# Even 11-step slots for the node work, and register reads and gathers issued one block earlier, in a graph and mixture-of-experts kernel

## What is computed

```
x = x + gat(layernorm(x), src, dst)     # 12 heads, softmax over incoming edges
x = x + moe(layernorm(x))               # 4 experts, the best one for each node
x = x + gcn(layernorm(x), edge_index)   # two graph convolutions
x = x + ffn(layernorm(x))               # 768 -> 384 -> 768, tanh gelu
```

## Time and profile before

| | us |
|---|---|
| median of 3 runs | 1054.82 |
| lowest and highest | 1052.24, 1055.24 |
| the profiled execution's own time | 1055.24 |
| its span in the profile | 1053.4 |
| outside the span | 1.84 |
| TensorE busy | 980.8 (93%) |
| VectorE busy | 607.2 (58%) |
| ScalarE busy | 287.9 (27%) |
| GpSimd busy | 60.0 (6%) |

### The profile page before, as it was taken

One profiled execution on the slowest core, in us unless ns is written; L12 is line 12 of the kernel. 1 busy time (PEld: TensorE's weight loads), 2 busy tenths in 40 slices (PEclk: granted clock), 3 DMA queues, 4 the chain that ended last, 5 costly groups with the idle time before them and its releaser, 6 DMA issues. The chain is left out here.

```text
span 1053.4 us, 15653 instructions
## 1 busy us (share of the span) xinstructions
PE 980.8 (93%) x5652; PEld 793.7 (75%) x5652; DVE 607.2 (58%) x1261; ACT 287.9 (27%) x782; POOL 60.0 (6%) x114
## 2 busy tenths in 40 slices
PE   7999998999999999958599994999999999999997
PEld 4777676999999999946366652666997557888785
DVE  8887897999999999985322225552111112232331
ACT  2444344454444554213011110221111112200100
POOL 2000000000000000012122211000000000000000
PEclk9999998999999999979699996999999999999999
DMA  6000010000000001528552236114200005000001
GB/s 156 2 1 1 5 49 1 24 26 24 24 34 37 24 24 43 127 81 283 174 177 92 89 147 197 57 44 162 71 1 1 0 1 146 1 30 30 28 3 60
DMA packets 25528, 65.26 MB, mean 62 GB/s; under 512 B 5720, under 2 KB 9572, under 8 KB 25344
## 3 DMA queue, kind: packets, MB, share of 16 engines
q1 hardware_dynamic: 22833, 54.13, 16.5%
q0 software_dynamic: 2080, 10.23, 2.9%
q10 hardware_dynamic: 559, 0.16, 0.1%
HBM read 47.74 MB, written 16.76 MB: 61 GB/s over the span
## 5 line engine op out<-in xcount | busy, mean ns | idle before, releaser
L809 PE MATMUL O<-X,masks 125*125 125x264 f32 x1200 | 279.6, 333 | 2.9 <-DVE masks L954 2.9
L806 PE MATMUL O<-X,CSR 125*125 125x132 f32 x1080 | 245.1, 227 | 0.0
L809 PEld LDWEIGHTS O<-X,masks 125*125 125x125 f32 x1200 | 222.2, 187 | 3.1 <-issue 3.1
L954 DVE SCALAR_TENSOR_TENSOR masks<-a2b,NA,CSR 125x375 fp32r<-125x375 f32 (+1 forms) x360 | 212.5, 645 | 8.3 <-PE O L809 5.9
L806 PEld LDWEIGHTS O<-X,CSR 125*125 125x125 f32 x1080 | 205.2, 190 | 0.0
L1879 DVE SCALAR_TENSOR_TENSOR UL<-pw,dinv,UH 125x768 fp32r<-125x768 f32 x20 | 20.4, 1018 | 111.4 <-ACT UH L1802 111.4
L1659 PE MATMUL pw<-W 128*125 128x384 f32 x240 | 81.6, 498 | 1.0 <-ACT W L1795 1.0
L424 PE MATMUL pc<-ohs_a,ohd 125*125 125x512 f16 x375 | 77.9, 347 | 1.6 <-DVE ohs_a L629 1.6
L1659 PE MATMUL pw<-region,xr_or_h 128*125 128x384 f32 x240 | 77.6, 486 | 0.0
L151 POOL TENSOR_TENSOR rstd<-rstd,minus_half 125x1 f32<-125x1 f32 x40 | 25.4, 636 | 843.8 <-DVEq L145 843.8
L1659 PEld LDWEIGHTS pw<-W 128*125 128x125 f32 x240 | 45.5, 193 | 32.3 <-issue 3.7
(11 more groups left out here) (237 smaller groups left out, 1384.3 us busy)
## 6 DMA issues: line engine op xcount, KB each, us to landing
a2b<-a_rows SPq DMA_DIRECT2D x12, 610.4 KB
W<-in_L_ffn_W SPq DMA_DIRECT2D x4, 1152.0 KB, 5.9
WM<-in_L_ffn_W SPq DMA_DIRECT2D x4, 1152.0 KB, 8.4
xr_or_h<-in_x SPq DMA_DIRECT2D x10, 336.0 KB
region<-in_x SPq DMA_DIRECT2D x2, 1680.0 KB
z_rows<-region SPq DMA_DIRECT2D x10, 336.0 KB
region<-y_rows SPq DMA_DIRECT2D x10, 336.0 KB
x_rows<-xr_or_h SPq DMA_DIRECT2D x10, 336.0 KB
```

The lines of the kernel that those rows point to most:

```text
L806: nc.tensor.matmul(O[0:P, bank, d - d0, 2 * DP:4 * DP], CSR[:, s, d * P:(d + 1) * P], X[:, buf, s, 4:6, :].rearrange("p k d -> p (k d)"), ...
L809: ins = nc.tensor.matmul(O[0:P, bank, d - d0, 0:4 * DP], kept, X[:, buf, s, 0:4, :].rearrange("p k d -> p (k d)"), start=s == 0, stop=s == ...
L954: nc.vector.scalar_tensor_tensor(masks[:, s, 0:(d1 - d0) * P], a2b[:, buf, d0 * P:d1 * P], NA1[:, s, bass.ds(h, 1)], CSR[:, s, d0 * P:d1 * ...
```

## The change

1. Slots have 11 steps each, counted from step 0; `z_of` moves from step 9 to step 10 of a slot.
2. The first three gathers and their two waits move into the gating block; the wait for gather 0 before gather 1 is removed.
3. TensorE reads the experts of 11 of 13 tiles at the end of the gating block, ScalarE all 13, VectorE 4. The rest follows after `turn_slots(0)` (TensorE, 2) and after `copy_slots(0)` (VectorE, 9). No reads are left in the loops.
4. `s_map`, which releases the gathers, is raised after both `slot_node` and the first `spare` instruction; `dinv` moves to after `slot_out`.

```diff
-            SLOT_START = [(k * WIN + 1) // 2 - PRE for k in range(2 * NT + 2)]
+            SLOT = 11
...
-                        k, at = slot_of(n)
+                        k, at = divmod(n, SLOT)          # on pe, act and dve
...
-                            if at == 9:
+                            if at == 10:
                                 z_of(k)
...
                     answer_inverse_sqrt(pool, gdeg[:, :])
+                    pool.wait_ge(s_zst, 16 * (2 * NT + 1))
+                    pool.wait_ge(s_map, 1)
+                    for j in range(SLOTS):
+                        gather(j)
...
                     ins.then_inc(s_tabd, 1)
+                    pe.wait_ge(s_eid, 1)
+                    for j in range(NS - 2):
+                        experts_pe.append(expert_of(pe, j))
...
+                    act.wait_ge(s_eid, 1)
+                    for j in range(NS):
+                        experts_act.append(expert_of(act, j))
...
-                    dve.wait_ge(s_ra, degrees)
-                    ch(nc.vector.tensor_tensor(dinv[:, :], gdeg[:, :], seen[:, :], ALU.mult))
...
-                    nc.vector.tensor_copy(slot_node[:, :], ptab[:, 0:16]).then_inc(s_map, 1)
-                    ch(nc.vector.scalar_tensor_tensor(spare[:, :], ptab[:, 0:16], 0.0, spare[:, :],
+                    ch(nc.vector.tensor_copy(slot_node[:, :], ptab[:, 0:16]),
+                       nc.vector.scalar_tensor_tensor(spare[:, :], ptab[:, 0:16], 0.0, spare[:, :],
                                                       ALU.is_equal, ALU.mult))
+                    dve.sem_inc(s_map, 1)
                     ch(nc.vector.tensor_tensor(slot_out[:, :], spare[:, :], ptab[:, 0:16], ALU.add))
+                    dve.wait_ge(s_ra, degrees)
+                    ch(nc.vector.tensor_tensor(dinv[:, :], gdeg[:, :], seen[:, :], ALU.mult))
+                    for j in range(NS - 9):
+                        experts_dve.append(expert_of(dve, j))
...
-                    pool.wait_ge(s_zst, 16 * (2 * NT + 1))
-                    pool.wait_ge(s_map, 1)
-                    gather(0)
-                    pool.wait_ge(s_xs[0], 16)
-                    for j in range(1, SLOTS):
-                        gather(j)
...
-                    pe.wait_ge(s_eid, 1)
-                    experts = [expert_of(pe, j) for j in range(2)]
+                    experts = experts_pe
                     turn_slots(0)
+                    for j in range(NS - 2, NS):
+                        experts_pe.append(expert_of(pe, j))
...
                     copy_slots(0)
+                    for j in range(NS - 9, NS):
+                        experts_dve.append(expert_of(dve, j))
```

More of the change, by code:

```diff
@@ L280, in last_use @@
                 return STEP_OF[t, g - EPT * t]
-            def slot_of(n):
-                k = max(k for k, first in enumerate(SLOT_START) if first <= n)
-                return k, n - SLOT_START[k]
             def node_tile(i):
@@ L554, in _ @@
                     for n, (t, c) in enumerate(STEPS):
-                        k, at = slot_of(n)
+                        k, at = divmod(n, SLOT)
                         if at == 0 and node_tile(k - 2) is not None:
@@ L1180, in program @@
             s_gc3, s_gt3 = sem("gates_copied"), sem("gates_turned")
+            experts_pe, experts_act, experts_dve = [], [], []
             with nc.Block() as block:
@@ L1494, in _ @@
                         if j + 2 < NS:
-                            experts.append(expert_of(pe, j + 2))
-                        if j + 2 < NS:
                             turn_slots(j + 2)
@@ L1501, in _ @@
                 def _(act):
-                    act.wait_ge(s_eid, 1)
-                    experts = [expert_of(act, j) for j in range(3)]
+                    experts = experts_act
                     for j in range(NS):
-                        if 1 <= j <= NS - 3:
-                            experts.append(expert_of(act, j + 2))
                         act.wait_ge(s_ht, j + 1)
@@ L1515, in _ @@
                 def _(dve):
-                    dve.wait_ge(s_eid, 1)
-                    experts = [expert_of(dve, j) for j in range(4)]
+                    experts = experts_dve
                     def copy_slots(j):
@@ L1554, in _ @@
                         take_out(j)
-                        if 4 + j < NS:
-                            experts.append(expert_of(dve, 4 + j))
         moe.close()
```

## The result

Slower, and by more than forecast: the median of four runs is 1065.86 us (1062.35 to 1067.75) against 1054.73 us (1052.24 to 1055.24), a ratio of 1.0096 with a 95% interval of 1.0078 to 1.0114. The forecast was 1061.0 us with a range up to 1064.5. The profiled execution took 1065.26 us, with a span of 1063.5. Of the changed kernel 31 executions are on record in all; their median is 1064.27 us (1061.81 to 1067.75), so it is some 9.5 to 11 us slower.

A forecast was written before the change was run, and what follows sets the result against it. TensorE was taken as the bound, busy nine tenths of nearly every slice. Counting block +6.7 us and handover -0.6 us gave +6.1 us: 1061.3 from the profiled 1055.24, forecast 1061 us, own range 1058.5 to 1063.5, wider range 1057 to 1064.5.

The forecast's parts named there:

- three stalls of 1.55 us: Counting block, steps 19, 40 and 103: no node work ahead while TensorE waits for ScalarE's copy of counts; 4.65 us.
- one of 2.0: Counting block, step 61: ScalarE's take for project(4,0) goes before the copy of the counts, so the stall is 2.0 us.
- one of 0.2: Counting block, step 82: project(6,0), 1.33 us, covers most of the copy of the counts and leaves 0.2 us.
- the old one: Counting block, step 124, start of tile 6: a stall of 1.55 us both before and after the change.
- The sum of 6.7 us: Counting block: stalls of 6.9 us less a gain of 0.2 in small waits make it 6.7 us longer.
- Rival 2: Counting block stalls mostly repaid and gather 0 alone setting the handover: 2.7 us, 1057.5 us, no tellable change; chance 0.13.
- `turn_z`'s small waits: Counting block: turn_z's second part waits for ScalarE, 1.6 us before, 1.8 after; nothing gained within -0.2 to +0.2 us.
- Forecast -0.6 us: Handover to the expert block: earlier gathers let TensorE begin at 510.1 to 510.2, a saving of 0.6 us.
- second form of rival 1: Handover: barrier holds GpSimd until its gathers land, TensorE begins 4 us later, about 1065.5 us; rival 1's chance 0.12.
- The start of the gathers: Handover: gather 0 issued at about 505.5, 0.3 us after spare ends near 505.20, for chain wait and semaphore.
- The bound of 0.38 us: Register reads, end of gating block: at most 0.38 us each, taken as 0.1, hidden behind the gathers.
- The rule that I had set against my bound: Handover: tensor_load floor of about 600 ns, ScalarE's 13 reads 7.8 us, handover loses 2.7 us, sum 1064.5.

The follow-up runs named there:

- e2: Kernel before with everything but the slots: early gathers, early register reads and the new VectorE order; 1059.15 us, ratio 1.0044.
- e3: Kernel before with the register reads early in the gating block but the gathers after the barrier as before; 1061.44 us, ratio 1.0067.
- e4: Kernel before with the three gathers early in the gating block and the register reads where they were; 1060.09 us, ratio 1.0049.
- e6: Kernel before with only gather 0 early in the gating block, gathers 1 and 2 and all reads as before; 1056.37 us, ratio 1.0011.
- e8: The reads-only kernel e3 with 13 further unused reads on ScalarE ahead of its 13; one run, 1066.49 us.
- e5_shift3: Kernel before with its own 10- and 11-step slots, every slot but the first begun three steps later; 1062.92 us, ratio 1.0079.
- e7_cover6: Kernel before with slot 11, the last half project, moved to step 124, the first of tile 6; 1053.61 us, ratio 0.9984.
- e1: Kernel before with the 11-step slots alone and z_of at step 10; 1061.94 us, ratio 1.0064.

## Why the prediction was wrong

**The counting block was right, step by step.** Forecast: three stalls of 1.55 us, one of 2.0, one of 0.2, the old one unchanged. Idle time shown: 1.39 us at steps 19, 40 and 103 as at 124, 1.75 at 61, and at 82 the tile goes on at 87.94, 0.2 us behind the 1.33 us of the project (86.39). Forecast of the waits for ScalarE: 6 to 7.5 us in five or six pieces; shown: 7.3 in five. The sum of 6.7 us came out as 6.1 against the profiled execution of before, or 6.6 us against kernels whose counting block is unchanged (L190 at 175.14 to 175.18 in e2, e3, e4, e6 and e8, against 181.77). e5_shift3 shows that the phase is the cause, and e7_cover6 that node work ahead of the tile is the cover. Rival 2, the stalls mostly repaid, needed `turn_z`'s small waits to go; they are still 1.0 us in six pieces.

**The handover was wrong in sign.** Forecast -0.6 us; measured +3.24 us in the trace. TensorE begins 9.10 us behind the cast; the forecast was 5.2 to 5.4, with 6 as the sign of being wrong. Of the 10.0 us between the two profiled executions 6.1 were forecast. The handover has 3.8 of the 3.9 us that were missed; the counting block came out 0.6 us lower and the rest of the program 0.7 higher. The step that failed is this one: "Issued 1.25 us apart, the third ends near 505.5 + 1.5 + 1.25 + 0.95 = 509.2. A barrier costs 0.92 us from last work to first. So TensorE begins at 510.1 to 510.2". I let GpSimd enter the barrier when the issue of its last gather was over. In every kernel with a gather ahead of the barrier (e2, e4, e6 and the change itself) the next block began only after the last gather had landed. In the changed kernel the third gather lands at 521.5, GpSimd's `DRAIN` ends at 521.7 and TensorE begins at 522.0. This is the second form of rival 1, to which I gave 0.12 with the note that the trace of before can't exclude it. Its time of 1065.5 us is 0.4 us from the one measured, in part by luck: it put 4.0 us on the handover, and the 0.7 us of the last paragraph of this section make up for most of the difference. The chance was too low. "No gather is in flight at a block's end before" was a reason to hold both cases open, not a reason for the cheaper one. The trace of before would have spoken for the dearer one. GpSimd's own `DRAIN` is in the view of the block's line, with ordinary work in flight, and the timeline has that work:

```profile
L1182 POOLq DRAIN  x1: 2071/2071/2071, 487.5 to 487.5; - x1
487.58 1.97 POOL L151 TENSOR_TENSOR gdeg<-gdeg,minus_half 125x10 f32<-125x10 f32 x1 [1.01 <-DVEq L145]
```

The `DRAIN` lasts until 489.6, when that work is over (487.58 + 1.97), not only until it is issued.

**The start of the gathers was mis-sized.** The release did come earlier, but gather 0 starts 0.95 us behind the end of `spare` (513.15 to 514.10), where I had put 0.3. The same gap is in e2_handover. I had split the 1.33 us of the earlier trace rows into 0.92 for the barrier and a small rest. The view of the block's line of the kernel before splits them the other way:

```profile
L1182 POOLq EVENT_SEMAPHORE  x2: 17/17/17, 505.7 to 505.8; - x2
```

The barrier opens 0.4 us behind the end of `slot_out` (505.37), and it takes another 0.9 us to the start of gather 0.

**The read was mis-sized too.** The bound of 0.38 us came from two block ends, 1.30 - 0.92. Measured: 0.53 us each on ScalarE and 0.66 on TensorE. The two ends have no common zero. At the one that I took off, the barrier opens at 464.4 (view of L747), 0.8 us behind the last work (463.61). At the other it opens at 174.5, 0.2 us behind it, and ScalarE's read with what follows it fills the rest (L303 is the line of the counting block, L750 that of the read; L1107 is `expert_of`, 505 to 508 us):

```profile
L303 POOLq EVENT_SEMAPHORE  x2: 17/17/17, 174.4 to 174.5; - x2
L750 ACTq TENSOR_LOAD <-flag x1: 497/497/497, 174.6 to 174.6; - x1
L1107 ACTq TENSOR_LOAD <-eid x3: 277/277/288, 505.9 to 507.0; - x3
```

The last line holds the price itself, in the trace of before: three reads of the expert block start 0.55 us apart. In the whole change this error costs nothing: ScalarE and TensorE are through at 519.8 and 520.1, GpSimd only at 521.7. Without the gathers (e3_reads) the reads alone hold the barrier and cost as much as the slots. The rule that I had set against my bound, of the Trainium skill's page DMA: Bandwidth & Descriptors, section Latency and other measured facts, a floor of about 600 ns for a `tensor_load`, was nearer to what these runs show. The load alone of an expert's number, 0.27 to 0.33 us in the rows of L1102 above, lies below that floor; there the measurement decides. The time that the prediction gave by this rule is off by a little: 1055.24 + 6.7 + 2.7 - 0.4 is 1064.2 us, not 1064.5.

**That the reads gain nothing in the loops** was right: ten steady tiles of the expert block take 87.28 us before (530.07 to 617.35) and in e2_handover (534.01 to 621.29).

**What is left, some 0.7 us net, goes at least in part with TensorE's clock.** Windows of the head block after its first matmul, of the kernel before:

```profile
176.75:182.12 5.37, 5.37 (x25) 5.37 (x26) 5.37 (x9) 5.21 (x18) 0.00 (x0) 0.50 0.01 3
182.12:190.00 7.88, 7.88 (x70) 7.88 (x70) 6.57 (x13) 1.20 (x4) 0.00 (x0) 0.99 0.00 0
```

and of the changed kernel:

```profile
182.88:191.00 8.12, 8.12 (x38) 8.12 (x39) 7.81 (x13) 5.20 (x18) 0.00 (x0) 0.50 0.01 2
191.00:200.00 9.00, 9.00 (x80) 9.00 (x80) 6.91 (x12) 1.66 (x5) 0.00 (x0) 1.00 0.00 0
```

With the same code the granted clock stays at 0.50, the lower level of 1.2 GHz, for 8.1 us instead of 5.4. Of the other differences in the table, -1.57 us at the end goes with an earlier rise in the graph block, where twelve matmuls take 5.49 us instead of 6.59. Such differences come without any change: the 31 executions of the changed kernel lie from 1061.81 to 1067.75 us, with a mean granted clock of 0.971 to 0.974 in those up to 1063.0 us and of 0.968 in those above 1066. And from the first mask to `slot_node`, code that no kernel changed except for the end of the gating block, the profiles show 329.05 us before, 330.90 after, 330.92 in e1 and 327.7 in e8. Whether the change also moves these rises stays open.

## What to carry to other kernels

Where a matmul must wait for the copy of its only accumulator, put independent work of about the copy's length directly ahead of it, and check any new schedule by its phase against these waits, not by how even it looks. Before moving a transfer ahead of a barrier, ask what the barrier waits for: if it is the landing, the transfer gains nothing, and every further one moves the barrier back. Where the timeline of a profile shows nothing, ask for the line of the block and of the read: what a sequencer does alone is there. Register reads are serial work on the engine that does them: they are free where that engine is ahead or waits anyway, and dear at the end of a block, where the slowest list holds all engines.

## What the runs showed of the hardware

- A block's end waits for GpSimd's indirect DMAs. GpSimd's `DRAIN` ended at 510.6 with one in flight that landed at 510.5 (e6_onegather), at 514.0 with three of which the last landed at 513.8 (e4_gathers), and at 521.7 with a last landing at 521.5 (the change).
- A read of a checked value from SBUF into a register took 0.53 us of ScalarE's list, 0.66 of TensorE's and 0.63 of VectorE's, and 13 further ones on ScalarE moved gather 0 back by 6.90 us, so they stand one after another.
- GpSimd's indirect DMA started 0.9 us behind what released it (the barrier at 505.8 before, the end of `spare` at 513.15 after), against 0.30 us from the end of one issue to the next.
- Of three gathers in a row the first landed 3.9 to 4.0 us behind its issue (e2_handover, e4_gathers) and the others 4.5 to 4.9 (the same and the change), against a median of 3.9.
